# A squared-attention mixer rewritten tile by tile and run as a side program of the attention edge stage

## The reference, cut to what matters

```python
x = x + _L3_gnn_ref(xn, edge_index, L3_gnn_W, L3_gnn_a) + _L3_mix_ref(xn[None], ...)[0]

# graph attention, 50,000 edges
h = x @ W
s = h @ a[:f_out]; t = h @ a[f_out:]
e = jnp.exp(-jax.nn.leaky_relu(s[src] + t[dst], ALPHA))
rowsum = jax.ops.segment_sum(e, src, num_segments=n)
h_prime = jax.ops.segment_sum(e[:, None] * h[dst], src, num_segments=n)
h_prime = jax.nn.relu(h_prime / rowsum[:, None])

# squared mixer
qkv = x @ W_qkv + b_qkv
q, k, v = jnp.split(qkv, 3, axis=2)
q = q - jnp.mean(q, axis=2, keepdims=True)
k = k - jnp.mean(k, axis=2, keepdims=True)
q2 = q * q; k2 = k * k
k2 = _l2_normalize(k2 / (jnp.sum(k2, axis=2, keepdims=True) + EPS_DIV), axis=-2)   # over the nodes
q2 = _l2_normalize(q2 / (jnp.sum(q2, axis=2, keepdims=True) + EPS_DIV), axis=-1)   # over a row
kv = jnp.einsum('bnc,bnd->bcd', k2, v)
t2 = jnp.einsum('bnc,bcd->bnd', q2, kv) / math.sqrt(N)
out = (v + t2) @ W_out + b_out
```

## Time and profile before

| | us |
|---|---|
| median of 3 runs | 7706.6 |
| lowest and highest | 7699.64, 7709.82 |
| the profiled execution's own time | 7706.61 |
| its span on the core | 7704.9 |

### The profile page before, as it was taken

How to read it: one execution, slowest core, us unless ns; L and a number is a source line. 1 busy time by engine, 2 the same in 40 slices (tenths; PEclk the granted TensorE clock), 3 DMA queues, 4 the chain that set the end, 5 groups by cost and what they waited for, 6 DMA issues and landing times. The chain is left out here.

```text
span 7704.9 us, 74434 instructions
## 1 busy us (share of the span) xinstructions
PE 4594.6 (60%) x18357; PEld 3419.3 (44%) x18357; DVE 3425.1 (44%) x7895; ACT 1891.0 (25%) x4727; POOL 3734.1 (48%) x3581
## 2 busy tenths in 40 slices
PE   0160666666664974778854915554469748875628
PEld 0030444444443761366643813332358636664515
DVE  6830777777776125433344143323621152224461
ACT  0000555555552210033311200001022114431201
POOL 0776777777771651077712637770034347770000
PEclk9985777777776987887766957776689967777659
DMA  0011444444441662233432323361046423362000
GB/s 36 14 52 28 123 121 123 121 123 125 120 124 40 205 168 72 114 103 103 100 30 61 92 65 105 105 97 23 3 153 191 148 70 103 104 92 25 1 20 17
DMA packets 391531, 677.74 MB, mean 88 GB/s; under 512 B 127759, under 2 KB 258093, under 8 KB 387656
## 3 DMA queue, kind: packets, MB, share of 16 engines
q0 software_dynamic: 188992, 431.92, 23.6%
q1 hardware_dynamic: 202170, 241.74, 9.7%
HBM read 591.29 MB, written 81.90 MB: 87 GB/s over the span
## 5 line engine op out<-in xcount | busy, mean ns | idle before, releaser
L905 POOL DMA_INDIRECT g0e_got<-g_table,g0e_rc x496 | 594.3, 1198 | 293.3 <-issue 156.8
L690 POOL DMA_INDIRECT g1e_got<-g_table,g1e_rc x496 | 489.4, 987 | 477.2 <-DMA g1e_rc<-rec_dst 326.4
L907 POOL DMA_INDIRECT g0e_keyed<-g_keys,g0e_rc x496 | 569.0, 1147 | 166.7 <-issue 166.7
L690 POOL DMA_INDIRECT g3e_got<-g_table,g3e_rc x496 | 491.7, 991 | 255.9 <-issue 146.5
L690 POOL DMA_INDIRECT g2e_got<-g_table,g2e_rc x496 | 474.1, 956 | 261.1 <-issue 147.4
L753 PE MATMUL g2e_pa<-g2e_got,g2e_placew 128*125 128x256 f32 x992 | 364.3, 533 | 321.9 <-issue 210.2
L257 POOL DMA_INDIRECT rec_dst<-bydst_rc,bydst_sloti x391 | 393.3, 1006 | 294.4 <-DVEq L449 175.6
L943 ACT ACTIVATE g0e_spaced<-g0e_spread 125x512 bf16<-125x512 f32 x992 | 499.1, 625 | 21.8 <-PE g0e_spread L979 18.6
L1849 PE MATMUL f_p<-f_w2s,f_hid 128*128 128x256 f32 (+1 forms) x2176 | 493.1, 383 | 12.6 <-ACT f_hid L1869 1.7
L1838 PE MATMUL f_p<-f_xt,f_w1s 128*128 128x256 f32 (+1 forms) x2176 | 491.1, 383 | 15.4 <-DMA f_b2s<-in_L_ffn_b 10.3
L969 PE MATMUL g0e_pt<-g0e_new,g0e_placet 125*128 125x8 f32 x992 | 207.3, 337 | 489.0 <-DVEq L1039 489.0
(11 more groups left out here) (597 smaller groups left out, 8756.6 us busy)
## 6 DMA issues: line engine op xcount, KB each, us to landing
f_w1s<-in_L_ffn_W SPq DMA_DIRECT2D x32, 1024.0 KB
f_w2s<-in_L_ffn_W SPq DMA_DIRECT2D x32, 1024.0 KB
g_table<-g1t_out SPq DMA_DIRECT2D x25, 1000.0 KB
f_w1s<-in_L_ffn_w SPq DMA_DIRECT2D x40, 512.0 KB
f_w2s<-in_L_ffn_w SPq DMA_DIRECT2D x40, 512.0 KB
f_results<-f_y SPq DMA_DIRECT2D x72, 256.0 KB
f_b2s<-in_L_ffn_b SPq DMA_DIRECT2D x80, 128.0 KB
f_rows<-XN SPq DMA_DIRECT2D x3, 3125.0 KB
```

Of the source, the lines that this page charges most:

```text
L690: pool.indirect_dma_start(got[:, g % GOTS, j, :], None, table, bass.IndirectOffsetOnAxis(rc[:, g * GT + j, idx:idx + 1], 0))\
L905: pool.indirect_dma_start(got[:, s, j, :], None, table, bass.IndirectOffsetOnAxis(rc[:, sl, j, R_IDX:R_IDX + 1], 0)).then_inc(got_in[s], 16)
L907: pool.indirect_dma_start(keyed[:, s, j, :], None, keys, bass.IndirectOffsetOnAxis(rc[:, sl, j, R_KEY:R_KEY + 1], 0)).then_inc(got_in[s], 16)
```

## The change

`squared_mixer` and its call go. A class `SquaredMixer` takes their place, whose `tensor`, `scalar` and `vector` are Python generators; `edge_stage` takes one as `side` and, at the end of each turn of each of the three engines, has it issue instructions up to its next `yield`. What a generator has left is issued after the last turn. The loads are issued by SyncE behind the edge records'.

The arithmetic is another. The mean of q and of k over a row is taken out of the weights and the bias beforehand. W_v times W_out is made once, so that one product gives [v | v W_out + bias] of a tile. The squared queries are turned and written over `R.XNT`, tile by tile. kv is accumulated over the tiles in two PSUM banks, kv times W_out is made once (M), and each tile's output is one product of the turned squared queries with M, scaled by the row's factor while it is added to X.

Counted in the turn number n of the edge loop, the side program is placed so:

| engine | preparation | tile t = 0..24 | closing | output of tile t |
|---|---|---|---|---|
| TensorE | n = 1, 2 | n = 4+3t: q and k (512 columns); 5+3t: kv of tile t-1; 6+3t: v (512 columns), two transposes | n = 81: kv of tile 24; 82: norms and M | n = 83+t |
| VectorE | n = 1 to 3 | n = 5+3t: add bias, square q; 6+3t: square k; 7+3t: add bias to v, add to X, add the fourth powers | n = 81, 82 | n = 83+t |
| ScalarE | | n = 6+3t: fourth power of q; 7+3t: evacuate; 8+3t: scale k, fourth power | n = 81 | |

With a side program `edge_stage` has half the PSUM banks: one for L730, one for L742, two for L753. Without one the banks for L730 are twice as large, and in the mode that needs no spreading they and the placement tiles are not allocated.

```diff
+    def sync(self, sp):
+        a = self.a
+        sp.dma_start(self.w[:, :, 0:3 * D], chunks_of(a["L3_mix_W_qkv"], 3 * D)).then_inc(self.loaded, 16)
+        sp.dma_start(self.wout[:, :, :], chunks_of(a["L3_mix_W_out"], D)).then_inc(self.loaded, 16)
+        sp.dma_start(self.bias[:, 0:3 * D], row_of(a["L3_mix_b_qkv"], P)).then_inc(self.loaded, 16)
+        sp.dma_start(self.bout[:, :], row_of(a["L3_mix_b_out"], P)).then_inc(self.loaded, 16)
...
+    def tensor(self, pe):
...
+        def context(t):
+            pe.wait_ge(self.b_taken, t + 1)
+            pe.wait_ge(self.k_normed, t + 1)
+            for m in range(KC):
+                last = pe.matmul(self.C[m][:, 0:D], self.vx[:, t % 2, m * 128:(m + 1) * 128], self.k2[:, t % 2, :],
+                                 start=(t == 0), stop=(t == NT - 1))
+            last.then_inc(self.kv_made, 1)
+
+        pe.wait_ge(self.prepared, 1)
+        for t in range(NT):
+            rows = slice(t * P, (t + 1) * P)
+            if t > 0:
+                pe.wait_ge(self.b_taken, t)
+            for c in range(KC):
+                last = pe.matmul(self.A[0:P, :], R.XNT[:, c, rows], self.w[:, c, 0:2 * D], start=(c == 0), stop=(c == KC - 1))
+            last.then_inc(self.a_made, 1)
+            yield
+            if t > 0:
+                context(t - 1)
+            yield
+            pe.wait_ge(self.a_taken, t + 1)
+            for c in range(KC):
+                last = pe.matmul(self.A[0:P, :], R.XNT[:, c, rows], self.w[:, c, 2 * D:4 * D], start=(c == 0), stop=(c == KC - 1))
+            last.then_inc(self.b_made, 1)
+            pe.wait_ge(self.q_squared, t + 1)
+            if t > 0:
+                pe.wait_ge(self.evacuated, t)
+            for c in range(KC):
+                last = pe.transpose(self.T[:, c * P:(c + 1) * P], self.sq[:, t % 2, c * 128:(c + 1) * 128], R.identf[0:P, 0:P])
+            last.then_inc(self.turned, 1)
+            yield
+        yield
+        yield
+        context(NT - 1)
+        yield
+        pe.wait_ge(self.k_added, NT)
+        pe.wait_ge(self.evacuated, NT)
+        for c in range(KC):
+            last = pe.matmul(self.T[:, c:c + 1], self.ksq[:, c * 128:(c + 1) * 128], R.onesf[0:P, 0:1], start=True, stop=True)
+        last.then_inc(self.ksum_made, 1)
+        pe.wait_ge(self.kv_copied, 1)
+        pe.wait_ge(self.b_taken, NT)
+        for m in range(KC):
+            for j in range(KC):
+                last = pe.matmul(self.A[:, m * D:(m + 1) * D], self.kvt[:, j, m * 128:(m + 1) * 128], self.wout[:, j, :],
+                                 start=(j == 0), stop=(j == KC - 1))
+        last.then_inc(self.m_made, 1)
+        yield
+        pe.wait_ge(self.m_ready, 1)
+        for t in range(NT):
+            to = (self.A, self.T)[t % 2]
+            if t >= 2:
+                pe.wait_ge(self.o_added, t - 1)
+            for c in range(KC):
+                last = pe.matmul(to[0:P, 0:D], R.XNT[:, c, t * P:(t + 1) * P], self.M[:, c, :], start=(c == 0), stop=(c == KC - 1))
+            last.then_inc(self.o_made, 1)
+            yield
...
+        def turned(t):
+            act.wait_ge(self.turned, t + 1)
+            act.activation(R.XNT[:, :, t * P:(t + 1) * P], self.T[:, 0:KC * P].rearrange("k (c p) -> k c p", p=P),
+                           ACT.Copy).then_inc(self.evacuated, 1)
+
+        def keys(t):
+            act.wait_ge(self.k_squared, t + 1)
+            if t >= 2:
+                act.wait_ge(self.kv_made, t - 1)
+            act.activation(self.k2[:, t % 2, :], self.sq[:, t % 2, D:2 * D], ACT.Copy, scale=self.rk[:, t:t + 1])
+            act.drain().then_inc(self.k_normed, 1)
+            if t >= 1:
+                act.wait_ge(self.k_added, t)
+            act.activation(self.k4[:, :], self.k2[:, t % 2, :], ACT.Square).then_inc(self.k_fourth, 1)
+
+        for t in range(NT):
+            act.wait_ge(self.q_squared, t + 1)
+            act.activation(self.junk[:, :], self.sq[:, t % 2, 0:D], ACT.Square, accum_out=self.s2[:, t:t + 1])\
+                .then_inc(self.q_summed, 1)
+            yield
+            turned(t)
+            yield
+            keys(t)
+            yield
+        act.drain()
+        act.activation(self.s2[:, :], self.s2[:, :], ACT.Sqrt).then_inc(self.rows_rooted, 1)
+        act.wait_ge(self.ksum_made, 1)
+        act.activation(self.kn[:, :], self.T[:, 0:KC], ACT.Sqrt).then_inc(self.ksum_rooted, 1)
...
+        def queries(t):
+            dve.wait_ge(self.a_made, t + 1)
+            dve.tensor_tensor(self.qk[:, :], self.A[0:P, :], self.bias[:, 0:2 * D], ALU.add)
+            dve.drain().then_inc(self.a_taken, 1)
+            if t >= 2:
+                dve.wait_ge(self.turned, t - 1)
+                dve.wait_ge(self.q_summed, t - 1)
+            q = self.qk[:, 0:D]
+            dve.scalar_tensor_tensor(out=self.sq[:, t % 2, 0:D], in0=q, scalar=1.0, in1=q, op0=ALU.mult, op1=ALU.mult,
+                                     accum_out=self.s1q[:, t:t + 1])
+            dve.drain().then_inc(self.q_squared, 1)
+
+        def values(t):
+            dve.wait_ge(self.b_made, t + 1)
+            if t >= 2:
+                dve.wait_ge(self.kv_made, t - 1)
+            dve.tensor_tensor(self.vx[:, t % 2, :], self.A[0:P, :], self.bias[:, 2 * D:4 * D], ALU.add)
+            dve.drain().then_inc(self.b_taken, 1)
+            x = node_tile(R.X, t)
+            dve.tensor_tensor(x, x, self.vx[:, t % 2, D:2 * D], ALU.add)
+            dve.drain()
+
+        def add_keys(t):
+            dve.wait_ge(self.k_fourth, t + 1)
+            dve.tensor_tensor(self.ksq[:, :], self.ksq[:, :], self.k4[:, :], ALU.add)
+            dve.drain().then_inc(self.k_added, 1)
+
+        def keys(t):
+            if t >= 2:
+                dve.wait_ge(self.k_normed, t - 1)
+            k = self.qk[:, D:2 * D]
+            dve.scalar_tensor_tensor(out=self.sq[:, t % 2, D:2 * D], in0=k, scalar=1.0, in1=k, op0=ALU.mult, op1=ALU.mult,
+                                     accum_out=self.rk[:, t:t + 1])
+            dve.drain()
+            dve.tensor_scalar(self.rk[:, t:t + 1], self.rk[:, t:t + 1], 1e-7, None, ALU.add)
+            dve.drain()
+            dve.reciprocal(self.rk[:, t:t + 1], self.rk[:, t:t + 1])
+            dve.drain().then_inc(self.k_squared, 1)
+
+        for t in range(NT):
+            queries(t)
+            yield
+            keys(t)
+            yield
+            values(t)
+            if t > 0:
+                add_keys(t - 1)
+            yield
+        yield
+        add_keys(NT - 1)
+        dve.wait_ge(self.kv_made, NT)
+        for m in range(KC):
+            dve.tensor_copy(self.kvt[:, m, :], self.C[m][:, 0:D])
+        dve.drain().then_inc(self.kv_copied, 1)
+        yield
...
+        dve.wait_ge(self.m_made, 1)
+        dve.drain()
+        for m in range(KC):
+            dve.tensor_scalar(self.M[:, m, :], self.A[:, m * D:(m + 1) * D], self.kn[:, m:m + 1], float(N) ** -0.5,
+                              ALU.mult, ALU.mult)
+        dve.drain().then_inc(self.m_ready, 1)
+        yield
+        for t in range(NT):
+            of = (self.A, self.T)[t % 2]
+            dve.wait_ge(self.o_made, t + 1)
+            x = node_tile(R.X, t)
+            dve.scalar_tensor_tensor(out=x, in0=of[0:P, 0:D], scalar=self.s2[:, t:t + 1], in1=x, op0=ALU.mult, op1=ALU.add)
+            dve.drain().then_inc(self.o_added, 1)
+            yield
...
+def edge_stage(nc, R, name, mode, b, acc, width, table, idx=R_IDX, spread=None, side=None, clear=True):
...
+    turns, adds = (2, 4) if side is None else (1, 2)
...
+            if side is not None:
+                side.sync(sp)
...
-                    if g >= 2:
-                        pe.wait_ge(evacuated, g - 1)
+                    if g >= turns:
+                        pe.wait_ge(evacuated, g - turns + 1)
...
-                        if j % each == 0 and x >= 4:
-                            pe.wait_ge(added, x - 3)
-                        last = pe.matmul(pa[x % 4][:, 0:width], placew[:, g % 3, j, :], got[:, g % GOTS, j, 0:width],
+                        if j % each == 0 and x >= adds:
...
+                advance(own)
+            run_out(own)
...
-        edge_stage(nc, R, "g3e", "gat", by_src, acc[:, :], W, table, spread=S[:, :])
+        with ExitStack() as inner:
+            edge_stage(nc, R, "g3e", "gat", by_src, acc[:, :], W, table, spread=S[:, :], side=SquaredMixer(nc, R, inner, a))
...
-def squared_mixer(nc, R, a):
...
         with nc.cleanup_on_exit():
-            squared_mixer(nc, R, a)
```

More of the change, by code:

```diff
@@ L659, in edge_stage @@
         coef2 = sb("coef2", [128, 4, GT])
-        pt = [ctx.enter_context(nc.psum_tensor(f"{name}_pt{k}", [P, 512], BF16)) for k in range(2)]
-        pq = [ctx.enter_context(nc.psum_tensor(f"{name}_pq{k}", [128, 64, 8], F32)) for k in range(2)]
-        pa = [ctx.enter_context(nc.psum_tensor(f"{name}_pa{k}", [P, 512], F32)) for k in range(4)]
+        if spreads:
```

(22 more changed lines are left out.)

243 lines of the change are left out of this document (121 added, 122 removed).

## The result

The changed kernel takes 7497.1 us (median of 4 runs, 7490.6 to 7505.0) beside 7708.2 us for the kernel before: a ratio of 0.9728, 95% interval [0.9711, 0.9744]. The forecast was 7476, its range 7424 to 7535.

What follows compares the result with a forecast made beforehand. The mixer lay wholly on the path; GpSimd's gathers paced the edge stage at 5.2 us a group, transfers near its end. Span 7704.9 - 297.3 + 67 (65 + 12 - 18 + 8) = 7474.6, forecast 7476 us, range 7424 to 7535.

Steps and rivals of the forecast that it cites:

- Part 1: Between the attention layer's last addition to X and the next layer's first statistics: removing the mixer saves 297.3 us.
- Part 2: Edge turns n = 4 to 78: the side program's tile work is hidden in 5.2 us turns, halved PSUM banks costing nothing.
- Part 3: Output turns n = 83 to 107: VectorE's same-turn wait makes turns serial, 8.2 us each; +65 us, bounds +24 to +109.
- with half of the time at each: Output turns: TensorE's clock taken as full half the time, half level otherwise, giving 7.9 us a turn from 6.55 and 9.95.
- the waiting between the dense parts grows: Output turns: the reason given for taking a turn as 8.2 us instead of 7.9.
- Part 4: Closing turns n = 81, 82: same-turn waits for kv and M make them serial; +12 us, bounds 6 to 20.
- Part 5: End of the edge stage, after group 107: 11 groups remain to be fetched instead of 14; -18 us, bounds 0 to -25.
- Part 6: Edge stage: late first gathers, +3 us, and GpSimd issues delayed by VectorE operations reading two SBUF operands, +5; +8 in all.
- 0.05 us for each of 100 operations: Edge stage: GpSimd delay priced per added VectorE operation with two SBUF operands, +5 us in all.
- All hidden: Rival: the clock stays full in output turns, 6.55 us each, and M is quick; 7421 to 7430 us, chance 0.12.
- TensorE bound in the tile turns: Rival: the grant stays at 0.77, tile turns take 6.35 us; 7546 us in total, chance of more than 7510: 0.20.
- The clock that is never granted: Rival: TensorE runs at 1.2 GHz in all turns, +437 us, total 7846, slower than before; chance 0.04.

## Why the prediction was right or wrong

The edge stage was to grow by 67 us and grew by 87.6, and the span came out at 7496.4 instead of 7474.6. The time, 7497.1, lies in the range that was given.

- **Part 1, the mixer removed (-297.3): right**, 322.2 - 24.9 = 297.3.
- **Part 2, tile turns hidden: right**, 436.4 us where 437.0 were. The reason held too: the grant was 0.97, and dense products beside each turn raise it (0.74 to 0.89 when they are added alone). That the banks cost nothing was shown alone (1.0001, second chip). The room is small, though: on the two slower chips, where plain turns take 5.9 us, the same turns cost 27 us. Why is open. TensorE's clock was lower there in the tile turns (0.87 on the second chip), and VectorE had waits that end with nothing local (last section); neither was tried apart.
- **Part 3, output turns (+65): mechanism right, size wrong**, +96.7, and this is the miss. All terms of the turn were good: VectorE's part 1.96 against 1.92, the turn at full clock 6.64 against 6.55, at half clock 9.6 to 10.0 for most against 9.95. What failed is the step "with half of the time at each". It took the share of all time at a level for the share of the work at it. The grant of 0.68 was not far from the 0.75 expected, and put into the forecast's formula (36% of the time at full clock) it gives 8.4 us, not 9.47. But the full clock fell on the waits, and 97% of the time of the edge sums was at the lower level. So nearly every turn was a slow one. The sentence "the waiting between the dense parts grows" saw the direction and gave it 0.3 us where it had 1.6 (9.47 - 7.9). With all turns slow the sum would have given 25 x 9.95 = 249, too much by 12, since in six of the 25 turns (8.2 to 8.7 us) the one-column products and the output product still had the full clock for most of their time, and the transposes had it nearly always.
- **Part 4, closing turns (+12): right in kind**, +8.6, inside 6 to 20. The sum counts three turns where two are serial; with two it gives 2 x 8.2 + 2.7 - 2 x 5.2 = 8.7. The loss exists only because serial turns follow: with the outputs a turn later it is caught up.
- **Part 5, given back at the end (-18): right**, -16.7. When group 107 was added, 14 logits were to come in both kernels. Before, all 14 waited for their gather; in the changed kernel the first five found it landed and nine waited, where the forecast had 11. So the adds first came 2.9 to 5.0 us apart, and only then the 6.6 forecast. The output-a-turn-later kernel shows it from the other side: there all 14 wait for their gathers again, and the same groups take 96.8 us.
- **Part 6, start and GpSimd (+8): too high**, about -1. The first gathers were not late (6297.02 against 6297.46), and the mean gather went from 991 to 988 ns. The 0.05 us for each of 100 operations was over four times too much: over the whole stage 19 gathers began inside one of the side program's VectorE operations with two SBUF operands, and cost 1.1 us together over 0.947 us each; the 77 that began inside L1111 cost 15.5 us, where 88 that began inside L809 had cost 18.1 before. The bound of 45 us, worked out from every operation delaying a gather by its whole length, was far from reached.
- **The rivals.** "All hidden" and "TensorE bound in the tile turns" did not occur on the chip of the forecast; a mild form of the second did on the two slower chips. The clock that is never granted is a half-truth: the work of the output turns had it that way, and only there. For all 102 turns it was excluded by the tile turns.

The miss of 21 us is 32 too little in part 3, less 3 too much in part 4 and 9 in part 6, and 1 each in part 5 and behind the edge stage, where the changed kernel is 1.1 us longer. The errors partly cancelled: that the number came so near is in part luck.

## What to carry to other kernels

When work is threaded into a skewed loop, look for every place where an engine waits for something made in the same turn: all that stands behind that wait in its queue, the next turn's work too, becomes serial. Moving the consumer by one turn costs no instruction and was worth 86 us of 7490 here. And read a mean granted clock together with where TensorE works: price a product at the clock that holds behind its wait, not at the mean of the stretch.

## What the runs showed of the hardware

- **Useless dense work can pay.** Two products of 512 columns in each wait of 2.0 us made 25 turns 67 us shorter. The clock fell behind waits of 2.0 us, with TensorE busy for 74% of the stretch (175.31 of 237.00); and it stayed at 0.97 with 92% busy (359.14 of 390.00).
- **Chips differed by 5.8% with the same kernel**, and in one respect in their traces. On the two slower chips plain edge turns of this stage mostly come in pairs of about 8.9 and 2.8 us, mean 5.9, where in the kernel before, on the chip of the forecast, they take 3.5 to 6.0 singly, 5.2 on average, until the transfers bound them. Waits of VectorE that end with nothing local show there, in the kernel with the side program after the loop (6737 to 7161):

```profile
DVE g_acc L1119 <- remote: 113.9, 26, 5.7
DVE g3e_coef L1087 <- remote: 60.1, 19, 6.2
```

  In the kernel before, on the faster chip, no such wait stands among VectorE's in the same turns. What it is was not settled.
- **A gather begun beside a large VectorE memset ended only behind it.** L1063 clears 125 x 6425 elements, and the stage's first gather, begun beside it, takes 5.40 us instead of 0.94, in the kernel before as well (5.39):

```profile
6296.10 5.41 DVE L1063 MEMSET g_acc<- 125x6425 f32 x1 [4.98 <-issue]
...
6297.02 5.40 POOL L986 DMA_INDIRECT g3e_got<-g_table,g3e_rc  x1 [92.47 <-DMA g3e_rc<-rec_src]
```

  The gather ends 0.9 us behind the memset, which is what it takes by itself. Two earlier stages of the kernel before show the same, with the gather begun at other points of the memset; this is one of them:

```profile
3248.61 5.39 DVE L761 MEMSET g_acc<- 125x6400 f32 x1 [1.78 <-issue]
...
3251.30 3.62 POOL L690 DMA_INDIRECT g1e_got<-g_table,g1e_rc  x1 [326.39 <-DMA g1e_rc<-rec_dst]
```

  In the other the gather takes 3.86 us. In all three it ends 0.9 us behind the memset, and the first gather of a stage whose memset was over takes 0.98 us, so it is not being the first that makes it long. No kernel without the memset was run.
